# Cross-attention and expert layer: turned copies of x and of the attention weights as inputs, the mean taken out of Wq, row sums from a column of ones, and the attention steps written out with two buffers

## What is computed

```
def _layernorm(x, eps=1e-05):
    return (x - mean(x)) / sqrt(var(x) + eps)

# cross attention, 64 keys for each of the 4 batches
q = layernorm(x) @ Wq.T + bq;  k = ctx @ Wk.T + bk;  v = ctx @ Wv.T + bv
x = x + softmax(q @ k.T) @ v

# experts: 8 experts, each takes the 256 tokens of a batch with its highest gate probability
xn = layernorm(x)
probs = softmax(xn @ gate_w)                       # (4, 1024, 8)
top_p, top_idx = top_k(probs.T, 256)
y = gelu(xn[top_idx] @ w1[e]) @ w2[e] * top_p
out = x + (y added at rows top_idx)
```

## Time and profile before

| | |
|---|---|
| median of three runs | 533.91 us (532.88 to 534.12) |
| the profiled execution's own time | 533.27 us |
| its span, first to last instruction | 531.5 us |
| granted TensorE clock, mean | 0.942 |
| busy: TensorE / VectorE / ScalarE / GpSimd | 478.5 / 314.8 / 221.5 / 202.6 us |
| attention: first instruction to the scaled logits (L929) | 0 to 73.67 us |
| routing: from there to the first product of an expert (L774) | 73.67 to 126.65 us |
| experts | 126.65 to 531.5 us |

### The profile page before, as it was taken

The page is one execution under the profiler, slowest core; times in us unless marked ns, Lnnn a source line. Parts: engine busy times, 40 slices in busy tenths (PEclk is TensorE's granted clock), DMA queues, the critical chain, the costliest instruction groups (busy, mean ns, idle before and its releaser), DMA issues.

```text
span 531.5 us, 10296 instructions
## 1 busy us (share of the span) xinstructions
PE 478.5 (90%) x3400; PEld 425.3 (80%) x3400; DVE 314.8 (59%) x827; ACT 221.5 (42%) x549; POOL 202.6 (38%) x167
## 2 busy tenths in 40 slices
PE   4999826539999999999999999999999999999990
PEld 3887715437899988998999899898989999999990
DVE  3588558988656555755576465557555764664430
ACT  1478869302234423542452344245424532552320
POOL 5354410015046316341814372255408242822304
PEclk9999965559999999999999999999999999999996
DMA  8922226102415243351517151623434170413213
GB/s 226 328 87 83 84 75 271 57 5 79 159 42 82 68 130 61 61 155 45 83 35 197 31 85 34 169 52 70 127 71 73 48 197 20 85 20 36 22 19 39
DMA packets 34098, 47.98 MB, mean 90 GB/s; under 512 B 3745, under 2 KB 29474, under 8 KB 33570
## 3 DMA queue, kind: packets, MB, share of 16 engines
q0 software_dynamic: 12288, 17.08, 18.3%
q1 hardware_dynamic: 21794, 30.71, 17.3%
HBM read 30.72 MB, written 16.92 MB: 90 GB/s over the span
## 4 chain that ended last, share of the span: by engine, by line
PE 78%; DVE 9%; ACT 5%; issue 2%; DMA 2%; SPq 2%; POOL 1%; ACTq 0%; DVEq 0%; POOLq 0%
PE wide L788 35%; PE bank L774 33%; PE bank L614 4%; PE bank L749 3%; DMA x_all<-in_x_dram 2%; ACT ysb L510 2%; DVE over L956 2%; ACT prb L516 2%; DVE floor L969 1%; POOL out_dram L437 1%; DVE cand L951 1%; DVE reached L963 1%; PE wide L721 1%; PE bank L691 1%; PE wide L614 1%
## 5 line engine op out<-in xcount | busy, mean ns | idle before, releaser
L788 PE MATMUL wide<-w2hi,hhi 128*128 128x256 f32 x512 | 148.3, 290 | 0.0
L437 POOL DMA_INDIRECT out_dram<-ysb,sidx x64 | 102.3, 1599 | 116.9 <-ACT ysb L575 101.0
L788 PE MATMUL wide<-w2hi,hlo 128*128 128x256 f32 x512 | 144.7, 283 | 0.0
L788 PE MATMUL wide<-w2lo,hhi 128*128 128x256 f32 x512 | 144.4, 282 | 0.0
L565 ACT ACTIVATE hraw<-bank 128x512 f32<-128x512 f32 x128 | 76.4, 597 | 142.3 <-PE bank L774 131.7
L429 POOL DMA_INDIRECT xg<-xn_rows,gidx x64 | 66.0, 1032 | 167.1 <-issue 119.0
L1109 DVE CAST hhi<-hraw 128x512 fp32r<-128x512 f32 x128 | 55.8, 436 | 97.6 <-ACT hraw L565 91.9
L788 PEld LDWEIGHTS wide<-w2hi,hhi 128*128 128x128 f32 x512 | 97.5, 190 | 3.7
L788 PEld LDWEIGHTS wide<-w2lo,hhi 128*128 128x128 f32 x512 | 96.6, 189 | 3.4
L788 PEld LDWEIGHTS wide<-w2hi,hlo 128*128 128x128 f32 x512 | 96.5, 188 | 0.0
L1111 DVE TENSOR_TENSOR hlo<-hraw,hhi 128x512 fp32r<-128x512 f32 x128 | 89.0, 696 | 4.4
(11 more groups left out here) (149 smaller groups left out, 531.4 us busy)
## 6 DMA issues: line engine op xcount, KB each, us to landing
w1raw<-in_L_ffn_w_dram SPq DMA_DIRECT2D x8, 1024.0 KB
w2raw<-in_L_ffn_w_dram SPq DMA_DIRECT2D x8, 1024.0 KB
xn_rows<-x_all SPq DMA_DIRECT2D x4, 1060.0 KB, 4.0
out_dram<-x_all SPq DMA_DIRECT2D x8, 512.0 KB, 2.9
x_all<-in_x_dram SPq DMA_DIRECT2D x3, 1024.0 KB, 10.4
x_all<-in_x_dram SPq DMA_DIRECT2D x2, 512.0 KB, 6.4
xg<-xn_rows,gidx POOLq DMA_INDIRECT x64
out_dram<-ysb,sidx POOLq DMA_INDIRECT x64
```

The lines of the kernel that those rows point to most:

```text
L437: pool.indirect_dma_start(out=out_rows, out_offset=at, in_=ysb[g][:, i, :], in_offset=None, compute_op=ALU.add).then_inc(rows_added, 16)
L788: t = pe.matmul(o, hh[s % 4][:, i * P:(i + 1) * P], w[:, j, :], start=(j == 0 and m == 0 and i % 2 == 0), stop=(j == HC - 1 and m == 2), s ...
```

## The change

- **Inputs.** The host passes more arrays: x turned (`x_turned`, 256 x 4 x 1024), the context, Wk and Wv turned, Wv also as it is, and one small array with bk, bq, bv and the gate weights.
- **Loads.** ScalarE issues five loads (context, small array, both forms of Wv, bv); SyncE issues Wk, Wq, and then in turn a turned group and a plain group of x, each 512 KB with a semaphore of its own. The turned x has room for four groups (`raw`); groups 4 to 7 are loaded when the scores of group 0 to 3 are done. `raw` shares its memory with `w1raw` and `w2raw`, so the first expert's weights are loaded only when all scores are done.
- **Centring.** The mean is taken out of the rows of Wq, once, by VectorE, instead of out of x. GpSimd's `xc`, TensorE's turns of x and ScalarE's `xcT` copies go; scores are computed from `raw`, one step earlier, into bank 0 or 1 by turns.
- **Row sums.** `v` has a 266th column of ones (VX), so the product with the values gives the row sums; the exponential has no accumulator, and the reciprocal is taken from `wide` at the head of the residual.
- **Mean.** `nm2` goes: ScalarE's square takes scale -1 and the new mean itself as bias.
- **Extra columns.** Copied out of PSUM by ScalarE, not VectorE.
- **Buffers and order.** `score`, `nmax` and `prb` have two buffers, and the twelve steps are all written out. `folded_keys` runs after step 0, `values` after step 1.

```diff
-            pe.wait_ge(consts, N_CONST)
-            pe.wait_ge(kv_loaded, 48)
-            for dst, src in ((bank[0], ctx_sb), (bank[1], wk_sb)):
...
+            pe.wait_ge(kv_loaded, 32)
             for m in range(KC):
...
+                t.then_inc(folded, 1)
+            pe.wait_ge(consts, N_CONST)
+            pe.wait_ge(small_loaded, 16)
...
+                pe.wait_ge(wq_ready, KC)
...
             def step(j):          # TensorE
-                if active(j, 2):
-                    g = j - 2
-                    pe.wait_ge(xcT_ready, KC * (g + 1))
...
                 if active(j, 3):
...
-                        t = turn(bank[3][0:S, i * P:(i + 1) * P], prb[:, i, :])
+                        t = turn(bank[3][0:S, i * P:(i + 1) * P], prb[g % 2][:, i, :])
...
                 if active(j, 1):
                     g = j - 1
-                    pe.wait_ge(xc_ready, g + 1)
-                    wait_count(pe, xcT_ready, KC * g)
-                    for k in range(KC):
-                        for i in range(GT):
-                            t = turn(bank[k][:, i * P:(i + 1) * P], xc[:, i, k * P:(k + 1) * P])
-                        t.then_inc(xc_turned, 1)
+                    pe.wait_ge(xT_loaded[g], 16)
+                    if g == 0:
+                        pe.wait_ge(qk_ready, 1)
+                    wait_count(pe, score_ready, g - 1)
+                    wait_count(pe, extra_ready, g - 1)
+                    for i in range(GT):
+                        for k in range(KC):
+                            t = pe.matmul(score_bank(g)[:, i], raw[:, g % 4, k, i * P:(i + 1) * P], qk[:, k, g // GB, :],
+                                          start=(k == 0), stop=(k == KC - 1))
+                    t.then_inc(scored, 1)
...
-                        t = pe.matmul(wide[:, i, 0:CX], prbT[:, i * P:(i + 1) * P],
-                                      v_sb[:, bass.ds(g // GB, 1), :], start=True, stop=True)
+                        t = pe.matmul(wide[:, i, 0:VX], prbT[:, i * P:(i + 1) * P], v_sb[:, g // GB, :], start=True, stop=True)
...
-            run_steps(pe, step, {1: folded_keys, 2: values, 4: odd_values})
+            run_steps(pe, step, {0: folded_keys, 1: values, 4: odd_values})
...
+            dve.wait_ge(q_loaded, 16)
+            dve.tensor_reduce(wq_mean[:], wq_sb[:], AX.X, ALU.add).then_inc(wq_summed, 1)
...
+            for k in range(KC):
+                dve.tensor_scalar(wq_sb[:, k], wq_sb[:, k], wq_mean[:, k:k + 1], None, ALU.subtract).then_inc(wq_ready, 1)
...
             def step(j):          # VectorE
                 if active(j, 4):
...
+                    dve.wait_ge(attended, g + 1)
+                    dve.reciprocal(rinv[:].unsqueeze(2), wide[:, :, CX:VX]).then_inc(rinv_ready, 1)
+                    dve.wait_ge(extra_ready, g + 1)
+                    dve.wait_ge(rinv_ready, g + 1)
+                    for i in range(GT):
                         dve.scalar_tensor_tensor(out=rows[:, i, :], in0=wide[:, i, 0:CX], scalar=rinv[:, i:i + 1],
                                                  in1=rows[:, i, :], op0=ALU.mult, op1=ALU.add).then_inc(x1_ready, 1)
-                    dve.wait_ge(x1_ready, GT * (g + 1))
-                    dve.scalar_tensor_tensor(out=columns_of(nm2, g).unsqueeze(2), in0=rows[:, :, C + E:CX], scalar=-1.0,
...
             def step(j):          # ScalarE
...
-                if active(j, 1):
-                    g = j - 1
-                    for k in range(KC):
-                        act.wait_ge(xc_turned, KC * g + k + 1)
-                        act.activation(xcT[:, k], bank[k][:], ACT.Copy).then_inc(xcT_ready, 1)
...
-                    act.wait_ge(extra_ready, g + 1)
...
                 if active(j, 2):
                     g = j - 2
+                    act.wait_ge(score_ready, g + 1)
+                    act.activation(extra_cols(g), score_bank(g)[:, :, S:SX], ACT.Copy).then_inc(extra_ready, 1)
                     act.wait_ge(max_ready, g + 1)
+                    wait_count(act, prb_turned, g - 1)
                     for i in range(GT):
-                        a = act.activation(prb[:, i, :], score[:, i, :], ACT.Exp, bias=nmax[:, i:i + 1],
-                                           accum_out=psums[:, i:i + 1])
+                        a = act.activation(prb[g % 2][:, i, :], score[g % 2][:, i, :], ACT.Exp, bias=nmax[g % 2][:, i:i + 1])
...
+            def load_turned(g):   # SyncE
+                sp.dma_start(raw[:, g % 4], xT_g[:, :, g // GB, g % GB * GP:(g % GB + 1) * GP]).then_inc(xT_loaded[g], 16)
+
+            for g in range(NG):
+                if g < 4:
+                    load_turned(g)
+                sp.dma_start(xcols(g), x_g[:, g // GB, g % GB]).then_inc(x_loaded[g], 16)
...
             def step(j):
+                if active(j, 1) and j - 1 + 4 < NG:
+                    sp.wait_ge(scored, j)
+                    load_turned(j - 1 + 4)
...
+            run_steps(sp, step, {2: odd_values, NG + 1: first_weights})
```

More of the change, by code:

```diff
@@ L43, in wait_count, with build @@
     eng.wait_ge(sem, n)
-def build(nc, x, ctx_in, Wq, bq, Wk, bk, Wv, bv, gate_w, w1, w2, out):
+def build(nc, x, xT, ctxT_in, Wq, WkT, Wv, WvT, bv, small, w1, w2, out):
     B, T, C = x.shape
-    S = ctx_in.shape[1]
+    S = ctxT_in.shape[1] // B
     E, _, H = w1.shape
@@ L123, in build @@
         qk_bias = sb("qk_bias", [P, B, S], F32)
[L124 to L125 removed]
+        v_sb = sb("v_sb", [S, B, VX], F32)
+        v_odd = sb("v_odd", [P, B // 2, VX], F32)
         x_all = sb("x_all", [P, B, TC, CX], F32)
@@ L130, in build @@
         ve1 = sb("ve1", [P, NC], F32)
+        raw = sb("raw", [P, 4, KC, GP], F32)
+        w1raw = raw[:, 0:2].rearrange("p a k n -> p (a k n)").rearrange("p (k h) -> p k h", k=KC)
+        w2raw = raw[:, 2:4].rearrange("p a k n -> p (a k n)").rearrange("p (j d) -> p j d", j=HC)
+        assert KC * H == 2 * KC * GP and HC * C == 2 * KC * GP
         rs1 = sb("rs1", [P, NC], F32)
-        nm1 = sb("nm1", [P, NC], F32)
         ysb = [sb(f"ysb{g}", [P, NL, C], F32) for g in range(NU)]
         assert NL == GT
[L135 to L140, removed]
+        sq = ysb[0]
+        score = [sb(f"score{i}", [P, GT, S], F32) for i in range(2)]
+        nmax = [sb(f"nmax{i}", [P, GT], F32) for i in range(2)]
+        prb = [sb(f"prb{i}", [P, GT, S], F32) for i in range(2)]
         prbT = sb("prbT", [S, GT * P], F32)
@@ L191, in build @@
         v_loaded = sem("v_loaded")
-        x_first = sem("x_first")
-        x_second = sem("x_second")
-        x_rest = sem("x_rest")
+        small_loaded = sem("small_loaded")
+        x_loaded = [sem(f"x_loaded{g}") for g in range(NG)]
+        xT_loaded = [sem(f"xT_loaded{g}") for g in range(NG)]
+        wq_summed = sem("wq_summed")
+        wq_ready = sem("wq_ready")
         consts = sem("consts")
@@ L281, in build @@
         LAST = 4
-        N_CONST = 13
+        N_CONST = 15
         def active(j, stage):
-            return not isinstance(j, int) or 0 <= j - stage < NG
+            return 0 <= j - stage < NG
         def run_steps(eng, body, after={}):
-            for j in range(LAST + 1):
+            for j in range(NG + LAST):
                 body(j)
@@ L293, in run_steps, with score_bank @@
                     after[j]()
[L294 to L299, removed]
+        def score_bank(g):
+            return bank[g % 2][:, 0:GT * SX].rearrange("p (i s) -> p i s", i=GT)
         def counts(h):
@@ L682, in step @@
             def step(j):
[L683 to L693 removed]
                 if active(j, 3):
                     g = j - 3
[L696 removed]
+                    if g == NG - 1:
                         keep_warm(bank[0], 8)
@@ L1180, in _, with layout, columns @@
             run_experts(dve, expert)
-_INS = ['x', 'ctx_1024', 'L0_xattn_Wq', 'L0_xattn_bq', 'L0_xattn_Wk', 'L0_xattn_bk', 'L0_xattn_Wv', 'L0_xattn_bv',
-        'L0_ffn_gate_w', 'L0_ffn_w1', 'L0_ffn_w2']
+def layout(inputs):
+    import numpy as _np
+    x = inputs['x']
+    ctx = inputs['ctx_1024']
+    Wk, Wv = inputs['L0_xattn_Wk'], inputs['L0_xattn_Wv']
+    gate = inputs['L0_ffn_gate_w']
+    B, T, C = x.shape
+    KC, TC = C // P, T // P
+    def columns(v):
+        return _np.reshape(v, (KC, P)).T
+    small = _np.concatenate([columns(inputs['L0_xattn_bk']), columns(inputs['L0_xattn_bq']), columns(inputs['L0_xattn_bv']),
+                             _np.reshape(_np.transpose(_np.reshape(gate, (KC, P, -1)), (1, 0, 2)), (P, -1))], axis=1)
+    return [('x', x),
+            ('x_turned', _np.reshape(_np.transpose(_np.reshape(x, (B, P, TC, C)), (3, 0, 2, 1)), (C, B, T))),
+            ('ctx_turned', _np.reshape(ctx, (-1, C)).T),
+            ('Wq', inputs['L0_xattn_Wq']),
+            ('Wk_turned', Wk.T),
+            ('Wv', Wv),
+            ('Wv_turned', Wv.T),
+            ('bv', inputs['L0_xattn_bv']),
+            ('small', small),
+            ('w1', inputs['L0_ffn_w1']),
+            ('w2', inputs['L0_ffn_w2'])]
 def kernel(**inputs):
@@ L1194 @@
```

(4 more changed lines are left out.)

190 lines of the change are left out of this document (67 added, 123 removed).

## The result

The changed kernel takes 541.2 us (median of six runs, 539.3 to 550.8) against 533.8 before: a ratio of 1.0138, 95% interval 1.0115 to 1.016. It is slower by 1.4% where 525 us was forecast. The profile taken with the result is one of 550.83 us (span 549.1).

What follows compares the result with a forecast made beforehand. TensorE holds 78% of the chain, mostly in untouched experts, so the start of the scaled logits was taken to decide. Gains of 3.6 + 4.0 + 1.0 = 8.6 us gave 524.7, stated as 525.0; 8-in-10 range 521.5 to 530.

Steps and rivals of the forecast that it cites:

- The front: From the start to the first residual: start moves from 29.97 to 26.4 us, 3.6 us gained.
- the sum: Whole kernel: gains of 3.6, 4.0 and 1.0 make 8.6 us, taking 533.27 to 524.7 us.
- the 1.2 us extra: Between start of `qk` and first scores: allowance for TensorE running partly at its slow speed, 1.2 us.
- The steps: Attention, first to last residual: seven steps shrink from 38.3 to 34.3 us, 4.0 us gained.
- the tail: Last residual to scaled logits: squares start earlier, 5.37 to 4.37 us, 1.0 us gained.
- term 2: Attention steps between residuals: work removed from each engine cuts 38.3 to 34.3 us, 4.0 us gained.
- The clock rival: Attention: TensorE drops to its lower clock for one step, 4.0 us longer, 529 us; chance 0.05.
- The loads rivals: Front and steps: late turned loads give 528 us (chance 0.12), or at 200 GB/s 537, slower than before (0.04).
- The covered work: First expert's w1 and w2 loads, issued at about 53 us instead of 12, and delayed stores: cost nothing.

Runs made afterwards that it cites:

- the first profile: Profile taken with the result, of an execution of the changed kernel as made, at 550.83 us.
- the second: Second profile, from running the changed kernel again without edit: profiled execution 539.6 us, median 543.7 us, ratio to before 1.0214.
- the profile with eight and three turns: Changed kernel plus identity turns before the exponential waits, eight in even groups, three in odd, twelve for group 6: median 530.4 us, profiled execution 524.57.
- the burst: Changed kernel plus twenty turns of the identity once, behind the scores of group 5: 538.5 us, ratio 1.0044.
- The thinned kernel: Kernel before, turning only one of four columns of x in each half from the third group on: median 553.5 us.
- the one with six: Changed kernel plus identity turns: eight behind first scores, six before exponential waits of groups 1 to 6, ten in group 6: 526.3 us, profiled execution 528.4.
- six turns everywhere: Changed kernel plus the identity turns of the one with six, and six also before the first exponential (group 0): 524.3 us, ratio 0.9838.

## Why the prediction was wrong

**The front came out right by two errors that cancel.** First scores 13.22 (12.75 in the first profile) for 13.3; first residual 26.52 in the second for 26.4. But TensorE started later than I had it, at 4.54 to 5.06 for 3.8, and with it `qk`, at 9.02 and 9.50 for 8.4. This agrees with the Trainium skill's rule on shared DMA engines (DMA: Bandwidth & Descriptors, Rules for kernel authors), which I left out of the sum: Wk landed 0.9 to 1.5 us after the 3.6 of the forecast, beside the 0.8 that I had estimated by that rule. And `qk` ran at the fast speed in both profiles, so that the 1.2 us extra that I had put in weren't needed. That the two are of one size is luck.

**The steps were right in their order and wrong in their clock.** With the clock held, the profile with eight and three turns comes near the forecast:

```profile
26.67 1.70 DVE L848 SCALAR_TENSOR_TENSOR x_all<-wide,rinv,x_all 128x265 f32<-128x265 f32 x4
31.45 1.69 DVE L848 SCALAR_TENSOR_TENSOR x_all<-wide,rinv,x_all 128x265 f32<-128x265 f32 x4
36.66 1.70 DVE L848 SCALAR_TENSOR_TENSOR x_all<-wide,rinv,x_all 128x265 f32<-128x265 f32 x4
...
60.39 1.69 DVE L848 SCALAR_TENSOR_TENSOR x_all<-wide,rinv,x_all 128x265 f32<-128x265 f32 x4
64.37 0.43 DVE L894 TENSOR_TENSOR logits<-x_all,rs 128x256 f32<-128x256 f32 x1 [1.12 <-POOL rs L411]
```

Forecast were 26.4, 30.9, 37.0, the last residual at 60.7 and the logits at 65.1. Seven steps take 33.7 (forecast 34.3), the tail 3.98 (4.37), and the time is 524.57 (524.7 from the sum). The single steps agree less well: two of them take 10.0 and not 10.65, and the one from the sixth residual to the seventh, at 51.43 and 56.19, takes 4.8 and not 3.6, so that part of the agreement is errors that cancel. In the changed kernel itself the first step took 4.8 and the next six 44.7 instead of 28.9 (from 31.30 to the last residual at 76.04): 15.8 us more, against 539.6 - 524.6 = 15.0 in the times. That is the whole miss of this execution; in the first profile the clock falls 18 us earlier, and the logits come another 10.7 us later.

**The step that failed** is in term 2, "what goes from a step: ... on TensorE eight turns of x", which I booked as nothing but relief: that the granted clock stays at 1.00 without these turns was a term put at nothing without a reason. The clock rival I priced at one step: "If it is down for one step, TensorE's 4.65 become 9.3 and the step is 4.0 longer: 529", with a chance of 0.05. Its parts:

- I had seen idle moments of 0.8 and 1.3 us in my schedule (0.66 and 1.33 came), and set them against the 2.7 us after which the clock fell at the end of the attention before. That row shows a fall after 2.7 us; it does not show that 1.3 us is safe. The runs show falls within or soon after idle moments of 0.66 (in one of the two profiles shown), 1.17, 1.33, 1.38 and 1.61 us. The kernel before could not have shown it: the longest idle moment between its scores and its last group was 0.68 us (60.87 to 61.55), and its clock stayed up. The right reading would have been a bound from one side only.
- I took it for granted that a busy TensorE gets its clock back within a step. It didn't for 68 us in the first profile (15.3 to 83.6). The price of one step was too high, since TensorE's 4.65 became 8.15 and not 9.3, some 3 us more than the 4.8 to 5.2 of a step with the clock held. But it is paid in every step that is left: 15.8 us from group 2 on, more than the 8.6 that were to be gained. So this was the rival that could decide the sign, and I had given that place to the loads.
- The section of the Trainium skill that the prediction cited on this (TensorE: Matmul & The Clock Gate, HAM oscillation) agrees with the falls in kind, waits inside a loop of products that put the clock back. But the waits here are for VectorE and ScalarE, not for a DMA, and they are far shorter than those of its example. What the same page says in The HAM clock gate, that activity releases the throttle, holds for the turns of the burst, but not for TensorE busy in 10.00 of 10.00 us with scores and values products. The measurement decides: the busy time that a profile prints does not tell whether the clock comes back.

**The loads rivals were wrong**: no wait of the steps is for a load, and half of the turned data less changed nothing in the best execution. **The covered work** cost at most 0.6 us: the logits' advance of 9.3 us in the profile with eight and three turns came through as 8.7 of the span.

**Still open** is what in the work of a step decides. The thinned kernel and the added turns change the idle time and the back-to-back work at once, so the runs don't separate the two. The length of one idle moment does not decide alone: the clock stayed at 1.00 through 0.68 us in the kernel before and through 0.66 in the profile with eight and three turns, and fell in the 0.66 of the one with six.

## What to carry to other kernels

Before taking work off TensorE, ask which idle moments that opens and what the granted clock does in the stages where the work is thin: here a moment of about a microsecond halved the clock for nearly all the steps behind it. Filling exactly these waits with six turns of the identity into a bank free at that time made 541.2 us 524.3 us, 0.7 under the forecast of 525.0; turns beyond the wait cost their own time (eight in each made a step 0.2 us longer). A kernel whose executions spread by 2%, as here, may be losing its clock in some of them; compare where the granted clock falls before calling it noise.

## What the runs showed that I had not expected

- The granted clock stays at 0.50 from 16 to 83 us with TensorE busy for 65.83 of these 67 us; its one long gap there is of 1.18 us, at 75.9.
- A second, smaller spread lies at the start: the eight instructions of `qk` take 1.97 us in some executions and 3.75 in others, with a granted clock of 1.00 in the rows of both. The first residual is then 2 us later and so is the end (profiles of 526.49, with six turns everywhere, and 524.57, with eight and three):

```profile
9.21 3.75 PE L626 MATMUL wide<-kT,wq_sb 128*128 128x256 f32 x8
```

```profile
9.54 1.96 PE L626 MATMUL wide<-kT,wq_sb 128*128 128x256 f32 x8
```

- Taking three quarters of the x turns of groups 2 to 7 out of the kernel before made it 3 to 27 us slower.
